# Attention layer on one core: the weighted sums of 8 heads in one run of the matrix engine instead of two runs of 4

## The chip, the core and the metric

One core of a Trainium2 chip runs the whole program. The time is the device time of one execution in microseconds (us). The engines are TensorE (PE), VectorE (DVE), ScalarE (ACT), GpSimd (POOL) and SyncE (SP, which only issues transfers).

## The reference

The input `x` is 8 sequences of 512 rows of 256. A first block (a small adapter with an expert matrix per sequence, a residual and a layer norm) is followed by a transformer layer with 16 heads of 16. Its attention adds a bias of 512 x 512 per head and masks columns:

```
x = _ln(src) * (1.0 + scale) + shift
scores = einsum('bhqd,bhkd->bhqk', q / sqrt(16), k) + attention_bias
scores = where(src_mask, -inf, scores)
ctx = einsum('bhqk,bhkd->bhqd', softmax(scores), v)
x = x + (ctx @ Wo + bo)
ff = _gelu2((_ln(x) * g2 + beta2) @ W1 + b1) @ W2 + b2
return x + ff
```

The weighted sums are the second `einsum`, `ctx`.

## The kernel before

**Tiling.** The 4096 rows are 16 chunks of 256 query rows (`NCH`, `CH`); a chunk is iteration `i`. A chunk has 16 heads x 2 halves of 128 queries = 32 score tiles of 128 x 512 (`TI`), one for each slot `t` of the iteration. Every engine has a program of its own, and all of them walk through the same slots.

**A score tile's way.** In slot `t` PE makes the scores (L823, bank `sc0` or `sc1`); DVE adds the masked bias and takes the maximum (L1371); ACT takes the exponential and its row sum (L996); three slots later (`LAG`), PE turns the tile in four transpositions (L830, bank `tp0` or `tp1`); ACT (L1002) or DVE (L1378, for the tiles in `DVE_MOVES`) copies it to `pT`. POOL has masked the bias earlier (L492). A score waits for the maximum of the tile two before it (L822), a turn for the exponential of its own tile and for the copy of the tile two before it (L827, L828). On ACT the copy of slot `t` (tile `t - 3`) stands ahead of the exponential of tile `t`; on DVE the maximum of tile `t` stands ahead of the copy.

**The weighted sums.** `pT` has two buffers of 4 heads (8 tiles, `TG`). `weigh(g)` (L777 to L791) takes one buffer: for 4 blocks of 128 keys and 4 heads it multiplies a 128 x 32 piece of `v_all` with a 128 x 256 piece of `pT`. The four heads stand in four column groups of the array (`tile_position`), so they run side by side. Even and odd groups of heads fill the two 16-row halves of each 32-row part of `pv[:, 0:256]`: the piece of `v_all` of an even group has its other 16 columns zero and the odd group adds. So two runs make one round `r` of 8 heads. In the profile a product of float32 shows as two records, so a run of 16 products has 32 records.

**Order around it.** Before, between and after the score and the turn of a slot (times `t.0`, `t.3`, `t.6`) each engine carries out other steps, whose slots are written in the tables `PE_AT`, `ACT_AT`, `DVE_AT`, `SP_AT`, `POOL_AT`, `MID` and `FFN` (L46 to L56). The runs of weighted sums stand on PE at 13.6, 21.6, 29.6 and, for the last group, 5.6 of the next iteration. Other steps on PE: `up` 0.3 (adapter), values 1.0 and 2.0, queries 8.6 and 10.0, transposition of the next rows `xm` 12.6, keys 15.6 and 16.3, `wo` 21.0 and 21.6, `ht` 28.6, and the feed-forward products in slots between. ACT: copy of the turned rows 14.0 (L859), queries 11.0 and 12.3, keys 17.0 and 18.0, a tanh at 5.0, 9.6, 14.3 and 19.0 (L957), `hT` 30.0. DVE: steps of two layer norms at 1.6 to 10.6 (ending in `xm`, L1110), gates of the feed-forward at 6.0, 10.3, 15.3, 19.6 (L1328), the output rows at 29.6 (L1335), the division of the weighted sums at 24.6 and 8.6 (L1349). POOL: inverse square roots at heads 6 and 8 of a chunk. SP loads the bias of head `n` after the turns of head `n - 8`. What an engine has in its list it does in that order; nothing overtakes.

**Waits of the weighted sums.** `weigh` waits for the copies of its 8 tiles, for `v_all`, and (first group of a round) for the division of the round before. It increments `pv_done`. The copies into a `pT` buffer wait until the run two groups back is done (L1001, L1377), the values' copy into `v_all` waits for the runs of the sequence two back (L1197), the division waits for the second run of its round (L1346). `spread_inverses` writes the other half of the bank of `pv` at 22.3 and 6.3 (4.0 in the last iteration).

Of the kernel before, what the change touches and what calls it, by code (L numbers as in the profile page):

```python
# [16 lines left out]
H, HD = 16, 16  # L17
# [3 lines left out]
CH = 256  # L21
NCH = B * S // CH
CT = D // P
FT = F // P
GH = 4
NG = H // GH
TI = 2 * H
TG = 2 * GH
KT = S // P
# [14 lines left out]


PE_AT = dict(up=0.3, v=(1.0, 2.0), q=(8.6, 10.0), xt1=12.6, k=(15.6, 16.3), down=(24.3, 25.3),  # L46
             pv=(13.6, 21.6, 29.6, 5.6), spread=(22.3, 6.3))
ACT_AT = dict(q=(11.0, 12.3), widen=(18.3, 2.3), spread=(23.6, 7.0), k=(17.0, 18.0), xT1=14.0, gelu=26.6)
DVE_AT = dict(x1=1.6, st0=2.3, mv0=2.6, v=3.0, n1=4.0, n2=6.3, st1=7.0, mv1=7.6, m1=8.3, m2=10.6, q=(11.6, 13.0),
              k=(17.6, 18.6), recip=(17.6, 1.6), ctx=(24.6, 8.6))  # L50
# [59 lines left out]
def wait(eng, sem, value):  # L110

    if value <= 0:
        return
    eng.wait_ge(sem, value)
# [7 lines left out]
def on_act(n):  # L122

    return n % TI not in (LAST_DVE_MOVES if n // TI == NCH - 1 else DVE_MOVES)


def moved(n, by_act):

    return sum(on_act(k) == by_act for k in range(n))


def head_of(hh):

    return 8 * (hh // 8) + 2 * (hh % GH) + hh // GH % 2
# [17 lines left out]
def build(nc, x, x_t, t_tok, e_tok, bias, mask, downT, upT, up_b, experts, gamma, beta,  # L152
# [16 lines left out]
    with ExitStack() as ctx:  # L169
        def sb(name, shape, dt=F32):  # L170
            return ctx.enter_context(nc.sbuf_tensor(name, shape, dt))

        def ps(name):
            return ctx.enter_context(nc.psum_tensor(name, [P, 512], F32))

        def sem(name):
            return ctx.enter_context(nc.semaphore(name))
# [26 lines left out]
        v_all = [sb(f"v_all{b}", [P, KT, HD + 2 * HD * H]) for b in range(2)]  # L204
        pT = [sb(f"pT{g}", [P, GH, KT, CH]) for g in range(2)]
# [58 lines left out]
        pv = ps("pv")  # L264
# [9 lines left out]
        def v_bank(c):  # L274
            return tp[1] if c == 0 else lb
# [34 lines left out]
        s = {n: sem(n) for n in names}  # L310
# [248 lines left out]
        def _(pe):  # L559
# [63 lines left out]
            def fold_expert(b, bank, j):  # L623
                return pe.matmul(bank[0:A + 1, j * D:(j + 1) * D], ew_t[:, b, :], up_w, start=True, stop=True)
# [23 lines left out]
            for b in range(6, 8):  # L648
                last = fold_expert(b, lc, b % 2)
# [24 lines left out]
            def body(i, attn, prev, nxt, pre, qv, down):  # L674
                a, c = i + 2, i + 1
                AT = PE_AT

                def norm_steps(t):
                    if pre and t == AT["up"]:
                        wait(pe, s["a_xt1"], a)  # L680
                        wait(pe, s["d_out"], i - 2)
                        adapter_up(a)
                    if qv and t in AT["q"]:
                        if t == AT["q"][0]:
                            pe.wait_ge(s["d_v"], c + 1)
                        queries(c, AT["q"].index(t))
                    if qv and t in AT["v"]:
                        if t == AT["v"][0]:
                            pe.wait_ge(s["a_xt1"], c + 1)
                            pe.wait_ge(s["d_k"], c + 1)  # L690
                            wait(pe, s["a_hT"], i - 1)
                        values(c, AT["v"].index(t))
                    if pre and t in AT["k"]:
                        if t == AT["k"][0]:
                            pe.wait_ge(s["a_xt1"], a + 1)
                            pe.wait_ge(s["d_q"], c + 1)
                        keys(a, AT["k"].index(t))
                    if pre and t == AT["xt1"]:
                        turn_rows(a)
                    if down and t in AT["down"]:  # L700
                        if t == AT["down"][0]:
                            wait(pe, s["d_act"], 4 * (i - 1))
                            pe.wait_ge(s["d_w1"], 1)
                        adapter_down((i + 3) // 2, AT["down"].index(t))
# [69 lines left out]
                        pe.wait_ge(s["d_hn"], m + 1)  # L774
                        transposes(lb, hn, "p_ht")

                def weigh(g):  # L777
                    gi = NG * i + g - (NG if g == NG - 1 else 0)
                    pe.wait_ge(s["copied_v"], moved(TG * (gi + 1), False))
                    pe.wait_ge(s["copied_a"], moved(TG * (gi + 1), True))  # L780
                    pe.wait_ge(s["d_v"], 2 * (gi // NG // 2) + 2)
                    if g % 2 == 0:
                        wait(pe, s["d_ctx"], gi // 2)
                    v = v_all[(gi // NG // 2) % 2]
                    for kt in range(KT):
                        for h in range(GH):
                            col = HD + 2 * HD * head_of(GH * g + h) - HD * (g % 2)
                            last = pe.matmul(pv[32 * h:32 * h + 32, 0:CH], v[:, kt, col:col + 2 * HD],  # L788
                                             pT[gi % 2][:, h, kt, :], start=(g % 2 == 0 and kt == 0),
                                             stop=(g % 2 == 1 and kt == KT - 1), tile_position=(0, 32 * h))  # L790
                    last.then_inc(s["pv_done"], 1)  # L791

                def spread_inverses(r):
                    ri = 2 * (i - r) + r
                    pe.wait_ge(s["a_wide"], ri + 1)
                    wait(pe, s["a_rin"], ri)
                    for j in range(2):
                        last = pe.transpose(inverse_bank(ri)[:, CH + j * P:CH + (j + 1) * P],
                                            rwide[:, j, :], ident[:, :])
                    last.then_inc(s["p_rin"], 1)  # L800

                def steps(t, at):
                    norm_steps(t)
                    if i == 1 and t in W1_AT["sums"]:
                        shift_sums(W1_AT["sums"].index(t))
                    for f in range(max(0, i - 2), min(i, NCH)):
                        ffn_steps(f, at)
                    if i > 0:
                        mid_steps(i - 1, at)
                    for g in range(NG):  # L810
                        if (prev if g == NG - 1 else attn) and t == AT["pv"][g]:
                            weigh(g)
                    for r in range(2):
                        if (prev if r else attn) and t == (4.0 if i == NCH else AT["spread"][r]):
                            spread_inverses(r)

                def score(t):
# [30 lines left out]
        def _(act):  # L848
# [83 lines left out]
            def body(i, attn, prev, nxt, pre, qv, down):  # L932
                a, c = i + 2, i + 1
                AT = ACT_AT
# [63 lines left out]

                def move(n):
                    act.wait_ge(s["pt_ready"], n + 1)  # L1000
                    wait(act, s["pv_done"], n // TG - 1)  # L1001
                    act.copy(pT[n // TG % 2][:, n // 2 % GH, :, (n % 2) * P:(n % 2 + 1) * P],  # L1002
                             tp[n % 2][:, :].rearrange("p (k q) -> p k q", k=KT)).then_inc(s["copied_a"], 1)

                for t in range(TI):
                    n = TI * i + t - LAG
# [7 lines left out]
        def _(dve):  # L1014
# [179 lines left out]
            def values(c):  # L1194
                b = c // 2
                dve.wait_ge(s["p_v"], c + 1)
                wait(dve, s["pv_done"], 2 * NG * (b - 1))  # L1197
                if c == 0:
                    dve.wait_ge(s["pool_chain"], 3)
                dst = v_all[b % 2][:, 2 * (c % 2):2 * (c % 2) + 2, HD:].rearrange("p j (h e) -> p j h e", e=2 * HD)  # L1200
                dve.tensor_tensor(dst[:, :, :, 0:HD],
                                  v_bank(c)[:, :].rearrange("p (j h d) -> p j h d", j=2, d=HD),
                                  bv_r[:, :].rearrange("p (h d) -> p h d", d=HD).unsqueeze(1).to_broadcast(
                                      [P, 2, H, HD]), ALU.add).then_inc(s["d_v"], 1)
# [43 lines left out]
            query_parts(0, 1)  # L1248
            dve.wait_ge(s["v_w_in"], 48)
            values(0)  # L1250
            shift_parts()
            for ft in range(FT):
# [4 lines left out]
            def body(i, attn, prev, nxt, pre, qv, down):  # L1257
                a, c = i + 2, i + 1
                AT = DVE_AT
# [83 lines left out]

                def divide(r):
                    ri = 2 * (i - r) + r
                    dve.wait_ge(s["pv_done"], 2 * ri + 2)  # L1346
                    dve.wait_ge(s["a_rin"], ri + 1)
                    wait(dve, s["p_wo"], i - r)
                    dve.tensor_tensor(ctxn[:, r, :], pv[:, 0:CH], rin[:, :], ALU.mult).then_inc(s["d_ctx"], 1)  # L1349
# [24 lines left out]

                def move(n):
                    dve.wait_ge(s["pt_ready"], n + 1)
                    wait(dve, s["pv_done"], n // TG - 1)  # L1377
                    dve.tensor_copy(pT[n // TG % 2][:, n // 2 % GH, :, (n % 2) * P:(n % 2 + 1) * P],  # L1378
                                    tp[n % 2][:, :].rearrange("p (k q) -> p k q", k=KT)).then_inc(s["copied_v"], 1)

                for t in range(TI):
                    n = TI * i + t - LAG
# [67 lines left out]
```

## Time and profile before

| | us |
|---|---|
| median of 3 runs | 959.73 (959.16 to 959.91) |
| profiled execution | 960.01 |
| its span, first to last instruction | 958.2 |
| PE busy | 890.0 (93%) |
| DVE busy | 703.1 (73%) |
| ACT busy | 703.9 (73%) |
| POOL busy | 702.8 (73%) |
| mean granted TensorE clock | 0.973 |

Busy time is the union of an engine's instructions; a matmul's end is modelled and overlaps the start of the next one, so what a product costs is best read from start to start. A step whose engine is idle much of the time costs nothing unless another engine waits for it. Idle time in brackets behind a row of the timeline names what the engine waited for. In a view by windows, the columns behind the window and its length are the busy times of PE, PEld (weight load), DVE, ACT and POOL (instructions in brackets), the granted TensorE clock, the share of the transfer engines and GB/s.

### The profile page before, as it was taken

How to read it: one execution, taken by the hardware profiler on the slowest of the kernel's cores; microseconds unless marked ns; L12 is line 12 of the kernel's file. 1: busy time of each engine (PE TensorE's matmuls, PEld its weight loads, DVE VectorE, ACT ScalarE, POOL GpSimd, SP SyncE). 2: the span in 40 equal slices, each digit the busy share in tenths (PEclk: the TensorE clock that was granted, in tenths of full speed). 3: DMA queues.
4: the chain of work that ended last, by engine and by line, in shares of the span. 5: the costliest groups of instructions: out<-in, count | busy, mean ns of one | idle time of the engine just before them, and what ended most of it. 6: DMA issues, size and time to landing. Idle time of an engine off the chain costs nothing. (4 is left out here: it accounts for less than half of the span.)

```text
span 958.2 us, 20699 instructions
## 1 busy us (share of the span) xinstructions
PE 890.0 (93%) x6472; PEld 659.6 (69%) x6472; DVE 703.1 (73%) x1901; ACT 703.9 (73%) x1667; POOL 702.8 (73%) x407
## 2 busy tenths in 40 slices
PE   3746889999999999999999999999999999999987
PEld 1425565777777776787777776787777777677765
DVE  4645787878778787878778787888778787675742
ACT  2435888978788787978788787978788787867641
POOL 1417997889788886978688886979788887885700
PEclk7877999999999999999999999999999999999998
DMA  5299969876897769776897769776897669765300
GB/s 158 79 263 335 293 221 256 241 237 200 254 290 206 230 210 255 238 238 198 249 291 209 231 208 270 228 238 200 245 267 214 220 195 274 238 192 166 100 12 11
DMA packets 147950, 207.41 MB, mean 216 GB/s; under 512 B 14385, under 2 KB 62322, under 8 KB 147842
## 3 DMA queue, kind: packets, MB, share of 16 engines
q1 hardware_dynamic: 145474, 204.12, 71.9%
q10 hardware_dynamic: 2368, 1.97, 0.8%
q8 instruction: 53, 0.87, 0.4%
q14 instruction: 55, 0.45, 0.2%
HBM read 185.05 MB, written 20.99 MB: 215 GB/s over the span
## 5 line engine op out<-in xcount | busy, mean ns | idle before, releaser
L492 POOL TENSOR_TENSOR bias_s<-mask_f,bias_s 128x1024 f32<-128x1024 f32 x256 | 601.2, 2372 | 132.5 <-DMA bias_s<-in_bias 132.2
L1371 DVE CUSTOM_DVE_ANT_0 bias_s<-sc,bias_s 128x512 f32<-128x512 f32 x512 | 347.6, 684 | 175.7 <-PE sc L823 165.3
L996 ACT ACTIVATE bias_s<-bias_s,mx 128x512 f32<-128x512 f32 x512 | 371.2, 725 | 91.4 <-DVE mx L1371 89.3
L830 PE MATMUL tp<-ident,bias_s 128*128 128x128 f32 x2048 | 311.5, 275 | 6.4 <-ACT pT L1002 3.4
L830 PEld LDWEIGHTS tp<-ident,bias_s 128*128 128x128 f32 x2048 | 252.1, 142 | 88.9 <-issue 15.0
L1002 ACT COPY pT<-tp 128x512 f32<-128x512 f32 x335 | 194.9, 582 | 100.6 <-PE tp L830 98.1
L823 PE MATMUL sc<-stk,stq 128*128 128x512 bf16 x512 | 196.4, 384 | 24.9 <-DVE mx L1371 14.2
L752 PE MATMUL la<-w_s,act_s 128*128 128x256 f32 x512 | 128.2, 380 | 0.2 <-DVE act_s L1328 0.2
L788 PE MATMUL pv<-pT,v_all 128*32 128x256 f32 x2048 | 124.3, 383 | 0.0
L1378 DVE COPY pT<-tp 128x512 f32<-128x512 f32 x177 | 121.1, 684 | 3.7 <-PE tp L830 3.6
L737 PE MATMUL lc<-hT,w_s 128*128 128x256 f32 x464 | 121.2, 385 | 2.5 <-ACT hT L951 1.9
L996 ACT ACTIVATION_READ_ACCUMULATOR bias_s<-bias_s,mx 128x1 f32 x512 | 98.4, 192 | 0.0
L823 PEld LDWEIGHTS sc<-stk,stq 128*128 128x128 bf16 x512 | 50.0, 98 | 66.5 <-issue 39.9
L752 PEld LDWEIGHTS la<-w_s,act_s 128*128 128x128 f32 x512 | 89.4, 190 | 8.4 <-DVE act_s L1328 0.4
L788 PEld LDWEIGHTS pv<-pT,v_all 128*32 128x32 f32 x2048 | 60.1, 110 | 49.0 <-issue 15.8
L737 PEld LDWEIGHTS lc<-hT,w_s 128*128 128x128 f32 x464 | 82.4, 193 | 12.9 <-ACT hT L951 2.5
L502 POOL TENSOR_SCALAR rs<-mv 128x2 f32<-128x2 f32 x48 | 9.3, 194 | 92.5 <-DVE mv L1105 90.1
L1328 DVE SCALAR_TENSOR_TENSOR act_s<-th,lc 128x512 f32<-128x512 f32 x57 | 39.0, 685 | 11.1 <-ACT th L957 10.8
L1371 DVE DVE_READ_ACCUMULATOR2_ANT mx<- 128x1 f32 x512 | 42.5, 83 | 0.0
L503 POOL TENSOR_TENSOR rs<-rs,powc 128x2 f32<-128x2 f32 x48 | 34.0, 708 | 4.0
L769 PE MATMUL lb<-wo_s,ctxn 128*128 128x256 f32 x128 | 33.0, 381 | 0.7 <-DVE ctxn L1349 0.7
L957 ACT ACTIVATE th<-lc 128x512 f32<-128x512 f32 x57 | 33.5, 587 | 0.0
(175 smaller groups left out, 797.1 us busy)
## 6 DMA issues: line engine op xcount, KB each, us to landing
bias_s<-in_bias SPq DMA_DIRECT2D x256, 512.0 KB, 4.6
stk<-k_parts SPq DMA_DIRECT2D x128, 96.0 KB, 3.9
stq<-q_parts SPq DMA_DIRECT2D x126, 96.0 KB, 4.1
k_parts<-kb SPq DMA_DIRECT2D x32, 192.0 KB, 2.3
q_parts<-qb SPq DMA_DIRECT2D x30, 192.0 KB, 2.4
xT<-in_x_t SPq DMA_DIRECT2D x8, 512.0 KB, 7.2
k_parts<-kb SPq DMA_DIRECT2D x32, 128.0 KB, 2.3
stk<-k_parts SPq DMA_DIRECT2D x64, 64.0 KB, 4.3
```

What stands on the lines that cost most here:

```text
L492: pool.tensor_tensor(tile, mask_f[:, :, :], tile, ALU.subtract).then_inc(s["masked"], 1)
L503: return pool.tensor_tensor(dst, dst, powc[:, :], ALU.pow)
L737: last = pe.matmul(h, w1_s[:, ct, ft * P:(ft + 1) * P], hT[:, ct, :], start=(ct == 0), stop=(ct == CT - 1))
L752: last = pe.matmul(rows, act_s[:, ft, j * P:(j + 1) * P], w2_s[:, ft, :], start=(ft == 0), stop=(ft == FT - 1))
L788: last = pe.matmul(pv[32 * h:32 * h + 32, 0:CH], v[:, kt, col:col + 2 * HD], pT[gi % 2][:, h, kt, :], start=(g % 2 == 0 and kt == 0), stop ...
L823: pe.matmul(sc[t % 2][:, :].rearrange("p (e k) -> p e k", e=2), stq[:, hh, j * P:(j + 1) * P], stk[:, :, hh, :], start=True, stop=True).th ...
L830: last = pe.transpose(tp[n % 2][:, kt * P:(kt + 1) * P], bias_s[:, n // 2 % NB, n % 2, kt * P:(kt + 1) * P], ident[:, :])
L996: act.activation(tile, tile, ACT.Exp, bias=mx[:, t:t + 1], scale=-1.0, accum_out=sums[:, j, head_of(hh):head_of(hh) + 1]).then_inc(s["prob ...
L1002: act.copy(pT[n // TG % 2][:, n // 2 % GH, :, (n % 2) * P:(n % 2 + 1) * P], tp[n % 2][:, :].rearrange("p (k q) -> p k q", k=KT)).then_inc( ...
L1328: dve.scalar_tensor_tensor(out=act_s[:, 2 * p:2 * p + 2, :].rearrange("p c n -> p (c n)"), in0=tanh_of(f, p), scalar=1.0, in1=w1_bank(f, p ...
L1371: dve.tensor_tensor_reduce(out=tile, in0=sc[t % 2][:, :], in1=tile, scale=1.0, scalar=BIG, op0=ALU.add, op1=ALU.min, accum_out=mx[:, t:t + ...
L1378: dve.tensor_copy(pT[n // TG % 2][:, n // 2 % GH, :, (n % 2) * P:(n % 2 + 1) * P], tp[n % 2][:, :].rearrange("p (k q) -> p k q", k=KT)).th ...
```

## The change

`weigh` takes a round of 8 heads: parts 0 and 1 (heads of `pT[0]`, then of `pT[1]`) one behind the other, 32 products in one run. It stands at 19.3 of its iteration and, for the second round, at 3.3 of the next. It waits for the copies of all 16 tiles. The very last round is split: its part 0 stands at 29.6 of the last chunk's iteration and its part 1 at 3.3 of the closing one. `pv_done` counts rounds instead of groups, and the waits on it are changed to match: a copy of tile `n` now waits for the round `n // 16` to be done. The inverses of the closing iteration stand on PE at 3.0 instead of 4.0.

```diff
 PE_AT = dict(up=0.3, v=(1.0, 2.0), q=(8.6, 10.0), xt1=12.6, k=(15.6, 16.3), down=(24.3, 25.3),
-             pv=(13.6, 21.6, 29.6, 5.6), spread=(22.3, 6.3))
+             pv=(19.3, 3.3), spread=(22.3, 6.3))
...
-                def weigh(g):
-                    gi = NG * i + g - (NG if g == NG - 1 else 0)
-                    pe.wait_ge(s["copied_v"], moved(TG * (gi + 1), False))
-                    pe.wait_ge(s["copied_a"], moved(TG * (gi + 1), True))
-                    pe.wait_ge(s["d_v"], 2 * (gi // NG // 2) + 2)
-                    if g % 2 == 0:
-                        wait(pe, s["d_ctx"], gi // 2)
-                    v = v_all[(gi // NG // 2) % 2]
-                    for kt in range(KT):
-                        for h in range(GH):
-                            col = HD + 2 * HD * head_of(GH * g + h) - HD * (g % 2)
-                            last = pe.matmul(pv[32 * h:32 * h + 32, 0:CH], v[:, kt, col:col + 2 * HD],
-                                             pT[gi % 2][:, h, kt, :], start=(g % 2 == 0 and kt == 0),
-                                             stop=(g % 2 == 1 and kt == KT - 1), tile_position=(0, 32 * h))
-                    last.then_inc(s["pv_done"], 1)
+                def weigh(ri, parts=range(2)):
+                    r, turned = ri % 2, TG * (2 * ri + parts[-1] + 1)
+                    pe.wait_ge(s["copied_v"], moved(turned, False))
+                    pe.wait_ge(s["copied_a"], moved(turned, True))
+                    pe.wait_ge(s["d_v"], 2 * (ri // 4) + 2)
+                    wait(pe, s["d_ctx"], ri)
+                    v = v_all[(ri // 4) % 2]
+                    for e in parts:
+                        for kt in range(KT):
+                            for h in range(GH):
+                                col = HD + 2 * HD * head_of(GH * (2 * r + e) + h) - HD * e
+                                last = pe.matmul(pv[32 * h:32 * h + 32, 0:CH], v[:, kt, col:col + 2 * HD],
+                                                 pT[e][:, h, kt, :], start=(e == 0 and kt == 0),
+                                                 stop=(e == 1 and kt == KT - 1), tile_position=(0, 32 * h))
+                    if parts[-1] == 1:
+                        last.then_inc(s["pv_done"], 1)
...
-                    for g in range(NG):
-                        if (prev if g == NG - 1 else attn) and t == AT["pv"][g]:
-                            weigh(g)
                     for r in range(2):
-                        if (prev if r else attn) and t == (4.0 if i == NCH else AT["spread"][r]):
+                        if (prev if r else attn) and t == AT["pv"][r]:
+                            weigh(2 * (i - r) + r, range(1, 2) if r and i == NCH else range(2))
+                    if i == NCH - 1 and t == 29.6:
+                        weigh(2 * i + 1, range(1))
+                    for r in range(2):
+                        if (prev if r else attn) and t == (3.0 if i == NCH else AT["spread"][r]):
                             spread_inverses(r)
...
                 def move(n):
                     act.wait_ge(s["pt_ready"], n + 1)
-                    wait(act, s["pv_done"], n // TG - 1)
+                    wait(act, s["pv_done"], n // (2 * TG))
...
-                wait(dve, s["pv_done"], 2 * NG * (b - 1))
+                wait(dve, s["pv_done"], NG * (b - 1))
...
-                    dve.wait_ge(s["pv_done"], 2 * ri + 2)
+                    dve.wait_ge(s["pv_done"], ri + 1)
...
                 def move(n):
                     dve.wait_ge(s["pt_ready"], n + 1)
-                    wait(dve, s["pv_done"], n // TG - 1)
+                    wait(dve, s["pv_done"], n // (2 * TG))
```

## Rows read from the trace of the kernel before

**Rows 1.** The page, part 1: busy us, share of the span, instructions.

```profile
PE 890.0 (93%) x6472; PEld 659.6 (69%) x6472; DVE 703.1 (73%) x1901; ACT 703.9 (73%) x1667; POOL 702.8 (73%) x407
```

**Rows 2.** Windows, one per chunk (0, 1, 8, 14, 15): length, then busy times, clock.

```profile
58.60:115.20 56.60, 42.87 (x278) 28.75 (x279) 35.88 (x99) 34.92 (x88) 40.49 (x22) 0.82 1.01 308
115.20:167.80 52.60, 48.14 (x354) 31.10 (x354) 42.09 (x115) 43.99 (x102) 46.16 (x27) 1.00 0.84 243
...
490.75:543.35 52.60, 52.23 (x402) 40.22 (x401) 42.64 (x116) 42.42 (x105) 44.80 (x26) 1.00 0.76 233
810.90:862.00 51.10, 49.73 (x386) 37.44 (x385) 36.11 (x96) 40.10 (x100) 41.61 (x21) 1.00 0.72 222
862.00:926.90 64.90, 61.93 (x444) 47.73 (x443) 39.04 (x100) 43.42 (x105) 31.47 (x16) 1.00 0.33 100
```

**Rows 3.** Waits of PE from 170 to 811 us: in total, times, longest.

```profile
PE la L563 <- DVE xm L1110: 3.9, 12, 0.3
```

**Rows 4.** Timeline of PE around a run (chunk 8): start, us, engine, line, operation.

```profile
511.96 1.03 PE L737 MATMUL lc<-hT,w_s 128*128 128x256 f32 x4
512.92 1.93 PE L788 MATMUL pv<-pT,v_all 128*32 128x256 f32 x32
514.79 0.39 PE L823 MATMUL sc<-stk,stq 128*128 128x512 bf16 x1
```

**Rows 5.** Timeline of three engines, slots 3 to 12.6 of chunk 8.

```profile
496.38 0.60 PE L830 MATMUL tp<-ident,bias_s 128*128 128x128 f32 x4
...
498.15 0.73 ACT L996 ACTIVATE bias_s<-bias_s,mx 128x512 f32<-128x512 f32 x1 [0.54 <-DVE mx L1371]
...
500.26 0.57 ACT L957 ACTIVATE th<-lc 128x512 f32<-128x512 f32 x1
...
506.29 0.69 DVE L1371 CUSTOM_DVE_ANT_0 bias_s<-sc,bias_s 128x512 f32<-128x512 f32 x1
...
509.02 0.87 DVE L1110 SCALAR_TENSOR_TENSOR xm<-la,rs,mod 128x256 f32<-128x256 f32 x2
...
509.95 0.66 PE L563 MATMUL la<-ident,xm 128*128 128x128 f32 x4 [0.33 <-DVE xm L1110]
```

**Rows 6.** Timeline of three engines, slots 13 to 19 of chunk 8.

```profile
513.01 0.68 DVE L1371 CUSTOM_DVE_ANT_0 bias_s<-sc,bias_s 128x512 f32<-128x512 f32 x1
...
514.46 0.56 ACT L859 COPY xT<-la 128x512 f32<-128x512 f32 x1
...
516.10 1.03 PE L589 MATMUL lb<-xT,wk_s 128*128 128x256 f32 x4
...
521.08 0.60 PE L830 MATMUL tp<-ident,bias_s 128*128 128x128 f32 x4
...
521.52 1.03 PE L752 MATMUL la<-w_s,act_s 128*128 128x256 f32 x4
...
522.14 0.59 ACT L1002 COPY pT<-tp 128x512 f32<-128x512 f32 x1
...
522.38 0.38 PE L823 MATMUL sc<-stk,stq 128*128 128x512 bf16 x1
```

**Rows 7.** Timeline of DVE and ACT behind the run at 21.6 of chunk 8.

```profile
529.47 0.69 DVE L1371 CUSTOM_DVE_ANT_0 bias_s<-sc,bias_s 128x512 f32<-128x512 f32 x1 [2.19 <-PE sc L823]
...
529.98 0.59 ACT L1002 COPY pT<-tp 128x512 f32<-128x512 f32 x1 [2.46 <-PE tp L830]
```

**Rows 8.** Timeline of DVE and PE from slot 29.6 of chunk 8 to slot 0.

```profile
541.22 0.68 DVE L1335 SCALAR_TENSOR_TENSOR outb<-la,x2s 128x512 f32<-128x512 f32 x1
...
542.50 0.69 DVE L1371 CUSTOM_DVE_ANT_0 bias_s<-sc,bias_s 128x512 f32<-128x512 f32 x1 [0.60 <-PE sc L823]
...
543.35 0.38 PE L823 MATMUL sc<-stk,stq 128*128 128x512 bf16 x1
```

## The prediction

> **What bounds the kernel now.** I read the page's busy times first: PE 93% of the span, VectorE (DVE) and ScalarE (ACT) 73% each [rows 1]. Then the windows by chunk [rows 2]: in a steady chunk (52.6 us here, 54.9 with an adapter product) PE is busy 52.2 us, ACT 42.4, DVE 42.6; chunk 0, chunk 1 and chunk 14 leave PE idle 13.7, 4.5 and 1.4 us. Then PE's waits over twelve steady chunks [rows 3]: 3.9 us in 641 us, all one wait of 0.3 us a chunk for `xm`. So PE sets the pace, and the others keep up. What matters is how narrowly: a score is allowed two slots ahead of its maximum, a transposed tile two ahead of its copy, so ACT and DVE can lag PE by about two slots and no more.
>
> **What the change removes.** Each run of weighted sums has an entry and an exit. In [rows 4] the product before the run starts at 511.96; four records of that size take 0.86 to 0.87 us start to start (521.52 to 522.38 in [rows 6]), 0.216 each, so the run could start at 512.825 and starts at 512.92: 0.095 us. From there, eight rounds of four heads at 0.216 us are 1.73 us, so the next score could start at 514.65 and starts at 514.79: 0.14 us. A run costs 1.97 us, of which 0.235 us is its two edges. Before there are 64 runs, after 33 (31 whole ones and the last one in two halves): 31 x 0.235 = 7.3 us less work for PE. The Trainium skill, "TensorEngine Tiling (Array Packing)", Key Properties, says that a change of tiling mode drains the engine; the trace agrees (the edges above). By that rule alone the change gains those 7.3 us; that is the first rival.
>
> **What it adds.** No arithmetic, no transfer, no instruction but fewer waits. It puts 16 rounds in one place: 16 x 0.216 + 0.235 = 3.69 us. The transposition of the next tile (16 or 0) is queued behind the run on PE, the next score behind that; at slot 3 ACT has the copy of tile 0 ahead of its next exponential, so ACT soon stands idle, and DVE gets no new score. The two tile buffers no longer alternate, but the copies don't wait for `pv_done`: PE turns tile 16 only after the run is over. The cost is elsewhere: the four old runs (slots 5.6, 13.6, 21.6, 29.6) were pauses in which ACT and DVE caught up. Where they had no slack, a pause taken away gives PE nothing. I follow chunk 8 through its four stretches [rows 5 to 8].
>
> Slots 3 to 12.6 (run at 5.6 gone) [rows 5]. The turn of tile 0 starts at 496.38; PE gets to the transposition of `xm` at 509.95. The chain to `xm`: tanh at 500.26 on ACT, the gate on DVE, then DVE without a pause (nine groups of instructions, none with idle time ahead) up to the maximum at 506.29, the exponential after it and the second tanh on ACT, its gate, `xm` at 509.02, PE at 509.95. From the first tanh that is 9.69 us, nearly all work. The first tanh is 3.88 us behind the turn of tile 0. In the new order the maximum of tile 3 is done during the run, so the 0.54 us that ACT waited at 498.15 falls away and tanh comes at 3.34 us. PE then waits until 3.34 + 9.69 - 0.06 = 12.97 us, against 13.57 before. Gain 0.60 of 1.97 us. (An earlier wait, of tile 4's turn for the copy of tile 2, lies within this one: PE would be there at 3.7 us, the copy, behind that tanh, ends at 4.4.)
>
> Slots 12.6 to 19.3 (run at 13.6 gone) [rows 6]. DVE is packed until the maximum at 513.01; its exponential follows, then the copy of the turned rows, from 514.46 to 515.02, and the key product at 516.10 needs it. Without the run PE would be there at 514.13, now at 515.06: gain 1.04. Then the run itself waits for the copy of tile 15: turn at 521.08, copy at 522.14 because a key conversion is ahead of it on ACT, its end at 522.73, while PE is done with the score at 522.60 and could enter at 522.69. The run enters near 522.81: 0.12 lost. Gain 0.92.
>
> Slots 19.3 to 29.6 (run at 21.6 gone) [rows 7]. DVE had 2.19 us and ACT 2.46 us idle around that run, and are rested by the run before. Tile 16's copy and the gate behind it on DVE cost 1.2 us, before the next score is in. Gain the full 1.97. Bounds: 0.9, if that start is worse than I read it, and 1.97.
>
> Slots 29.6 to 3.3 (run at 29.6 gone) [rows 8]. DVE is packed (maximum, copy, maximum, copy, output row at 541.22). The maximum that follows sat 0.60 us idle until 542.50 for a score; now it starts at 541.83, ends 0.70 later, and the first score of the next chunk, which needs it, starts at 542.55 in place of 543.35. Gain 0.80.
>
> Sum of a steady chunk: the removed pauses give back 0.60 + 0.92 + 1.97 + 0.80 = 4.29 us; the two runs at 3.3 and 19.3 cost 2 x 3.69 = 7.38. The chunk gets **3.09 us longer**, though PE has 0.47 us less to do.
>
> The ends, bounded from rows 2 and the same reasoning. Chunk 0 has no run at slot 3, PE idles 13.7 us anyway, and three runs (5.9 us) turn into one: +1.5, between 0 and 4. Chunk 1 has PE idle already, so its pauses give back less: +4, between 3 and 5.5. Chunk 14 prepares no chunk, its DVE is less loaded (36.1 of 51.1 us [rows 2]): +1.6, between 0.5 and 3. Chunk 15 prepares nothing at all, PE is busy 61.9 of 64.9 us and ACT 43.4 [rows 2], and its last run stays split: -0.5. The tail waits for the same last copy, then one half run as before: 0. Sum: 1.5 + 4 + 12 x 3.09 + 1.6 - 0.5 = 43.7 us on the profiled execution's 960.0 (span 958.2), so 1003.7; the median of the runs is 0.3 lower: **1003.4 us**.
>
> Covered at nothing: POOL's masks (44.8 of 52.6 us busy, with a longer chunk to do them in), the SP queue's loads (a tile is loaded long before its score), the inverses and divisions, whose runs end earlier than before (19.3 for 21.6, 3.3 for 5.6) with their own slots unchanged. If POOL's cover went, its price would be at most its idle time, 7.8 us a chunk, spread over waits that DVE hardly has today. The granted clock is 1.00 in all steady chunks and 0.82 in chunk 0 [rows 2], where PE idles most; a shift there may cost or give 2 us, which is in the range.
>
> **The rivals.**
>
> *The slack is enough, only the edges count.* For it: DVE and ACT are idle a fifth of every chunk, and PE shows no wait for them [rows 1 to 3]. Then it ends at 960.0 - 7.3 - 0.3, about 952.4 us. It decides if the new waits stay under 0.47 us a chunk. Against it: the chain of rows 5 has hardly any idle time in it for 9.7 us, and PE already waits at its end. Chance 0.07; 0.01 that gain and waits cancel within 0.2%. The skill's "Perfetto Trace Analysis" tells to take the engine with the most occupied time as the bottleneck; that points to this rival, and the rows of rows 5 are why I don't follow it.
>
> *One stretch binds, the others don't.* If ACT and DVE use the long run better than I read (less queued behind tile 16's and tile 0's copies), only slots 3 to 12.6 cost: +1.37 - 0.47 = 0.9 us a chunk, about 14 us in all: 974 us. Chance 0.14.
>
> *The gap after a long run spreads.* If ACT and DVE start each stretch too far behind, the one I count as a full gain gives back nothing either: 7.38 - 2.32 = 5.06 us a chunk, 12 x 5.06 + 7 = 68: 1028 us. Chance 0.10.
>
> *Nothing changes.* The code does what it says: one `start` and one `stop` per region of `pv`, the waits consistent. The order on PE is fixed by hand, so the runs can't stay apart. Chance under 0.01, within the 0.01 above.
>
> **How the numbers follow.** Forecast 0.68, with 985 to 1018 for itself (0.8 us a chunk either way and the ends' bounds). The range takes in most of the second rival's upper half: 978 to 1019. About 0.2% (1.9 us) is what a measurement of this kernel can tell from no change: faster 0.07, same 0.01, slower 0.92.
>
> **What would show it.** In the profile after: 33 runs, whole ones of 3.69 us start to start, PE busy some 7 us less in sum and idle some 50 us more; a steady chunk of about 55.7 us (58 with the adapter product). Waits of PE that are new: the turn of tile 4 on the copy of tile 2 (0.6 to 0.8 us), the rows of `xm` (about 1.3 in sum with it), the key product on ACT's copy of the turned rows (0.7), score 0 on DVE's maximum (0.8), the run at 19.3 on the copy of tile 15 (0.1). ACT and DVE idle about 3 us in each long run. Wrong would be: chunks under 54 us (the slack is there), or PE waiting in slots 20 to 29 as well (the gap spreads).

## The result and the profile after

| | before | after |
|---|---|---|
| median of the runs | 959.82 us (4 runs) | 1014.74 us (4 runs, 1011.95 to 1018.15) |
| ratio, 95% interval | | 1.0563, 1.0536 to 1.0591 |
| profiled execution, span | 960.01, 958.2 us | 1018.15, 1016.4 us |

The change makes the kernel 54.9 us slower; forecast was 43.6 us (1003.4, range 978 to 1019). The profiled execution is the slowest of its four, so its sums come to 58.2 us.

The page of the kernel after, parts 1 and 5 (busy us, share, count; in part 5 the idle time of PE before a group and what ended it):

```profile
PE 905.1 (89%) x6472; PEld 668.8 (66%) x6472; DVE 703.3 (69%) x1901; ACT 698.1 (69%) x1667; POOL 703.0 (69%) x407
...
L834 PE MATMUL tp<-ident,bias_s 128*128 128x128 f32 x2048 | 313.4, 276 | 33.0 <-ACT pT L1006 17.8
L827 PE MATMUL sc<-stk,stq 128*128 128x512 bf16 x512 | 196.2, 384 | 30.8 <-DVE mx L1375 18.5
L789 PE MATMUL pv<-pT,v_all 128*32 128x256 f32 x2048 | 119.0, 384 | 4.0 <-issue 3.1
L589 PE MATMUL lb<-xT,wk_s 128*128 128x256 f32 x120 | 32.2, 392 | 8.5 <-ACT xT L863 8.5
```

No engine has more to do: the counts are those of [rows 1], DVE is as busy as before and ACT 5.8 us less. PE waits now: before turns 33.0 us (before the change 6.4), before scores 30.8 (24.9), before keys 8.5 (0.5). The run itself is cheaper: its group is busy 119.0 us, where it was 124.3. That PE shows 905 us busy in place of 890 is no added work either; the last section comes back to it.

Windows by chunk of the kernel after (0, 1, 8, 14, 15), to be held against [rows 2]:

```profile
63.10:120.90 57.80, 41.64 (x247) 28.41 (x247) 35.71 (x99) 34.84 (x88) 42.71 (x23) 0.85 0.94 290
120.90:178.40 57.50, 48.45 (x353) 31.37 (x354) 42.00 (x115) 43.42 (x101) 44.16 (x26) 1.00 0.83 243
...
521.90:578.00 56.10, 53.15 (x402) 40.67 (x401) 42.75 (x116) 42.63 (x107) 43.17 (x26) 1.00 0.70 210
862.70:916.30 53.60, 50.17 (x385) 37.52 (x385) 35.91 (x96) 39.68 (x99) 40.86 (x21) 1.00 0.69 203
916.30:984.50 68.20, 64.00 (x476) 48.79 (x476) 39.21 (x100) 43.36 (x104) 32.17 (x16) 1.00 0.32 97
```

Every steady chunk is longer by the same amount: 56.1 us for 52.6 (even), 58.3 for 54.9 (odd). The granted clock is 1.00 in all of them, as before; it plays no part.

**The stretches.** I cut a chunk at four points on PE: the start of tile 0's turn, of the transposition of `xm`, of tile 16's turn, and of the score of tile 29. The same cut is made in every trace below. (From the rounded times of [rows 5] the first stretch before comes to 13.57 us.)

| stretch (chunk 8; odd chunk 9 in brackets) | before | after | difference | forecast |
|---|---|---|---|---|
| turn 0 to rows | 13.56 (13.56) | 12.88 (12.88) | -0.68 | -0.60 |
| rows to turn 16, with the run at 19.3 | 12.65 (12.65) | 15.55 (15.55) | +2.90 | -0.92 + 3.69 = +2.77 |
| turn 16 to score 29 | 16.73 (19.03) | 14.81 (17.11) | -1.92 | -1.97 |
| score 29 to turn 0, with the run at 3.3 | 9.66 (9.66) | 12.72 (12.93) | +3.06 (+3.27) | -0.80 + 3.69 = +2.89 |
| chunk | 52.60 (54.90) | 55.95 (58.47) | +3.35 (+3.57) | +3.09 |

Now the rows behind it. Timeline of three engines, kernel after, from the run at 3.3 to the rows of chunk 8; it answers to [rows 5]:

```profile
527.85 3.66 PE L789 MATMUL pv<-pT,v_all 128*32 128x256 f32 x64
...
531.44 0.66 PE L834 MATMUL tp<-ident,bias_s 128*128 128x128 f32 x4
...
532.13 0.59 ACT L1006 COPY pT<-tp 128x512 f32<-128x512 f32 x1 [3.66 <-PE tp L834]
...
533.35 0.69 DVE L1375 CUSTOM_DVE_ANT_0 bias_s<-sc,bias_s 128x512 f32<-128x512 f32 x1 [3.07 <-PE sc L827]
...
534.85 0.59 ACT L961 ACTIVATE th<-lc 128x512 f32<-128x512 f32 x1
...
536.06 0.63 PE L834 MATMUL tp<-ident,bias_s 128*128 128x128 f32 x4 [0.69 <-ACT pT L1006]
...
540.74 0.68 DVE L1375 CUSTOM_DVE_ANT_0 bias_s<-sc,bias_s 128x512 f32<-128x512 f32 x1
...
543.38 0.63 PE L834 MATMUL tp<-ident,bias_s 128*128 128x128 f32 x4 [0.39 <-ACT pT L1006]
543.39 0.87 DVE L1114 SCALAR_TENSOR_TENSOR xm<-la,rs,mod 128x256 f32<-128x256 f32 x2
...
544.32 0.66 PE L563 MATMUL la<-ident,xm 128*128 128x128 f32 x4 [0.31 <-DVE xm L1114]
```

ACT and DVE stand idle 3.66 and 3.07 us in the run. The first tanh comes 3.41 us behind the turn of tile 0 (3.88 before; forecast 3.34), and from it to the rows it takes 9.47 us (9.69 before). PE meets that chain three times: tile 4's turn waits 0.69 us, tile 9's 0.39 (a wait that was not forecast), the rows 0.31.

Timeline of three engines, kernel after, slots 13 to 19 of the same chunk, to be held against [rows 6]:

```profile
548.82 0.56 ACT L863 COPY xT<-la 128x512 f32<-128x512 f32 x1
...
549.44 1.13 PE L589 MATMUL lb<-xT,wk_s 128*128 128x256 f32 x4 [0.49 <-ACT xT L863]
...
554.52 0.60 PE L834 MATMUL tp<-ident,bias_s 128*128 128x128 f32 x4
...
555.58 0.59 ACT L1006 COPY pT<-tp 128x512 f32<-128x512 f32 x1
...
555.82 0.38 PE L827 MATMUL sc<-stk,stq 128*128 128x512 bf16 x1
...
556.27 3.66 PE L789 MATMUL pv<-pT,v_all 128*32 128x256 f32 x64
...
559.86 0.66 PE L834 MATMUL tp<-ident,bias_s 128*128 128x128 f32 x4
```

The keys wait for the copy of the rows, and the run starts 0.45 us behind the score, where a run that waits for nothing starts 0.31 behind one (0.216 and the edge of 0.095): 0.14 for the copy of tile 15, forecast 0.12. From its start to the next turn the run takes 3.59 us; with its entry edge 3.69, as forecast.

Slots 29 to 0 of the same chunk, to be held against [rows 8], and, in the first three rows, the odd chunk before it (ACT and PE, slots 26.6 to 30):

```profile
516.56 1.28 ACT L856 ACT_TABLE_LOAD   x1
...
518.56 1.28 ACT L1000 ACT_TABLE_LOAD   x1
...
520.72 0.66 PE L834 MATMUL tp<-ident,bias_s 128*128 128x128 f32 x4 [1.17 <-ACT bias_s L1000]
...
576.57 0.68 DVE L1339 SCALAR_TENSOR_TENSOR outb<-la,x2s 128x512 f32<-128x512 f32 x1
...
577.16 0.68 DVE L1375 CUSTOM_DVE_ANT_0 bias_s<-sc,bias_s 128x512 f32<-128x512 f32 x1
...
578.00 0.38 PE L827 MATMUL sc<-stk,stq 128*128 128x512 bf16 x1 [0.58 <-DVE mx L1375]
```

In the even chunk score 0 waits for the maximum behind the output rows, as forecast. In the odd chunk it is another resource that holds PE: the adapter's gelu makes ACT load two function tables of 1.28 us, the exponential of tile 27 is late, and its turn waits 1.17 us. Before, with the run at 29.6, the loads cost nothing: the stretch is 9.66 us in even and odd chunks.

### The profile page after: what moved, and what is told of

Read it like the earlier page. It is cut to its first block and busy times, and to the rows that moved or that the text cites. A ratio compares the mean times of both kernels' runs of the same rounds, so it can differ in the third digit from the quotient of the medians.

```text
span 1016.4 us, 20669 instructions
## 1 busy us (share of the span) xinstructions
PE 905.1 (89%) x6472; PEld 668.8 (66%) x6472; DVE 703.3 (69%) x1901; ACT 698.1 (69%) x1667; POOL 703.0 (69%) x407
## 3 DMA queue, kind: packets, MB, share of 16 engines
q10 hardware_dynamic: 2368, 1.97, 0.7%
## 5 line engine op out<-in xcount | busy, mean ns | idle before, releaser
L834 PEld LDWEIGHTS tp<-ident,bias_s 128*128 128x128 f32 x2048 | 244.8, 141 | 135.4 <-issue 56.9
L827 PE MATMUL sc<-stk,stq 128*128 128x512 bf16 x512 | 196.2, 384 | 30.8 <-DVE mx L1375 18.5
L789 PE MATMUL pv<-pT,v_all 128*32 128x256 f32 x2048 | 119.0, 384 | 4.0 <-issue 3.1
L789 PEld LDWEIGHTS pv<-pT,v_all 128*32 128x32 f32 x2048 | 69.7, 111 | 52.0 <-issue 19.1
L589 PE MATMUL lb<-xT,wk_s 128*128 128x256 f32 x120 | 32.2, 392 | 8.5 <-ACT xT L863 8.5
```

The lines of the kernel that those rows point to most:

```text
L827: pe.matmul(sc[t % 2][:, :].rearrange("p (e k) -> p e k", e=2), stq[:, hh, j * P:(j + 1) * P], stk[:, :, hh, :], start=True, stop=True).th ...
L834: last = pe.transpose(tp[n % 2][:, kt * P:(kt + 1) * P], bias_s[:, n // 2 % NB, n % 2, kt * P:(kt + 1) * P], ident[:, :])
```

## Experiments

All times are medians; ratios are to the kernel before, measured on the same chip. "Stretches" are the four lengths of the table, chunk 8.

**1 and 2: one round merged at a time.**

```diff
-             pv=(13.6, 21.6, 29.6, 5.6), spread=(22.3, 6.3))
+             pv=(19.3, 19.3, 29.6, 5.6), spread=(22.3, 6.3))
```

> The kernel before with only the first round of a chunk merged: both of its runs stand back to back at 19.3, the runs at 29.6 and 5.6 stay. Theory (what is lost is the pauses in stretches where ACT and DVE have no slack, and each stretch has its own price): the two stretches that this round touches cost 15.55 - 12.65 = +2.90 us and 14.81 - 16.73 = -1.92 us in the traces of before and after, so +0.98 us a chunk, about +15 us: 975 us (970 to 980). Rival (a long run of PE starves ACT and DVE by itself, wherever it stands): half of the whole loss of 55 us, 987 us. Rival (only the edges of runs count, the loss is elsewhere): 16 edges fewer, 956 us.

```diff
...
-                    for g in range(NG):
-                        if (prev if g == NG - 1 else attn) and t == AT["pv"][g]:
-                            weigh(g)
+                    for g in range(2):
+                        if attn and t == AT["pv"][g]:
+                            weigh(g, False)
+                    if prev and i < NCH and t == 3.3:
+                        weigh(2, True)
+                        weigh(3, True)
...
```

> The kernel before with only the second round of a chunk merged: both of its runs stand back to back at 3.3 of the next chunk, the runs at 13.6 and 21.6 stay; the last round stays as it was. Theory (each stretch has its own price): 12.88 - 13.56 = -0.68 us in slots 3 to 12.6 and about 12.79 - 9.66 = +3.13 us from slot 29 to the next turn of tile 0, so +2.45 us a chunk, 15 rounds, about +37 us: 997 us (990 to 1002). Rival (a long run starves ACT and DVE by itself): 987 us. Rival (only edges count): 956 us.

Measured: first round merged 977.21 us, 1.0171 (1.0137 to 1.0206); second round merged 993.87 us, 1.0337 (1.0305 to 1.0370). Stretches 13.56, 15.41, 14.81, 9.72 and 12.88, 12.65, 16.73, 12.65. The two losses (17 and 34 us) are not alike, and together make 51 of the 55 us. Each touches only its own two stretches, and these have the lengths of the kernel after to within 0.14 us (15.41 for 15.55 the widest). So the loss goes by the place, not by the number of long runs.

**3: `xm` ahead of the gate.**

```diff
-DVE_AT = dict(x1=1.6, st0=2.3, mv0=2.6, v=3.0, n1=4.0, n2=6.3, st1=7.0, mv1=7.6, m1=8.3, m2=10.6, q=(11.6, 13.0),
+DVE_AT = dict(x1=1.6, st0=2.3, mv0=2.6, v=3.0, n1=4.0, n2=6.3, st1=7.0, mv1=7.6, m1=8.3, m2=10.3, q=(11.6, 13.0),
...
-FFN = dict(hT=30.0, w1=(3.0, 4.0, 8.0, 9.0, 13.0, 13.6, 17.6, 18.3), tanh=(5.0, 9.6, 14.3, 19.0),
+FFN = dict(hT=30.0, w1=(3.0, 4.0, 8.0, 9.0, 13.0, 13.6, 17.6, 18.3), tanh=(5.0, 10.3, 14.3, 19.0),
```

> The changed kernel with two steps moved in slots 9.6 to 10.6: DVE makes xm (10.3) ahead of the second gate (10.3, behind it) instead of after it, and ACT's second tanh goes from 9.6 to 10.3, behind the copy of tile 7. Theory: the rows' transposition waits for xm in that order only because the gate waits for the tanh; it comes up to 0.97 us earlier, but the next stretch is bound by DVE's maxima and ACT's copy of the turned rows, which come only 0.33 us earlier, so most of it is given back: -0.33 to -0.5 us a chunk, about 1009 us (1005 to 1013). Rival (the long run itself is the loss): no change, 1014 to 1015. Rival (PE paced by this wait alone): -0.97 us a chunk, 1001.

Measured 1015.36 us, 1.0574 (1.0525 to 1.0623), against 1.0563 for the changed kernel: nothing gained. Stretches 11.94, 16.42, 14.81, 12.65: the rows come 0.94 us earlier, and the next stretch is 0.87 us longer. PE's timeline in that kernel, slot 15 of chunk 8:

```profile
546.90 0.39 PE L827 MATMUL sc<-stk,stq 128*128 128x512 bf16 x1 [0.49 <-DVE mx L1375]
547.13 0.60 PE L834 MATMUL tp<-ident,bias_s 128*128 128x128 f32 x4
548.22 1.13 PE L589 MATMUL lb<-xT,wk_s 128*128 128x256 f32 x4 [0.49 <-ACT xT L863]
```

PE came earlier and waited more: now also for DVE's maximum of tile 13, and then for ACT's copy as before. My expectation of 1009 us (1005 to 1013) missed: I counted 0.33 us for DVE's packed list being started earlier and got 0.07. A wait on the bound engine is not a price; what it shields has to be free too.

**4: the copy of the turned rows ahead of an exponential.**

```diff
-ACT_AT = dict(q=(11.0, 12.3), widen=(18.3, 2.3), spread=(23.6, 7.0), k=(17.0, 18.0), xT1=14.0, gelu=26.6)
+ACT_AT = dict(q=(11.0, 12.3), widen=(18.3, 2.3), spread=(23.6, 7.0), k=(17.0, 18.0), xT1=13.3, gelu=26.6)
```

> The changed kernel with ACT's copy of the turned rows moved from 14.0 to 13.3, ahead of the exponential of tile 13 that waits for its maximum. Theory: the key product waits 0.49 us for this copy (its start 0.65 us later than PE could); with the copy done, that wait is gone and no other stands in its place at once: -0.5 to -0.65 us a chunk, about 1006 us (1003 to 1010). Rival (the long run itself, or the entry wait at 19.3 behind the key conversions takes it over): no change, 1013 to 1015.

Measured 1006.87 us, 1.0473 (1.0436 to 1.0510), 8 us under the changed kernel. The second stretch is 14.79 for 15.55 us, the others are unchanged, and the keys' wait is gone. So this wait was a price by itself, as forecast; per chunk it was 0.76 us where I had 0.5 to 0.65.

**5: the output rows later.**

```diff
-PE_AT = dict(up=0.3, v=(1.0, 2.0), q=(8.6, 10.0), xt1=12.6, k=(15.6, 16.3), down=(24.3, 25.3),
+PE_AT = dict(up=0.6, v=(1.0, 2.0), q=(8.6, 10.0), xt1=12.6, k=(15.6, 16.3), down=(24.3, 25.3),
...
-           gate=(6.0, 10.3, 15.3, 19.6), w2=(19.0, 20.0, 23.6, 24.6, 25.6, 26.0, 27.0, 28.0), out=29.6, store=31.0)
+           gate=(6.0, 10.3, 15.3, 19.6), w2=(19.0, 20.0, 23.6, 24.6, 25.6, 26.0, 27.0, 28.0), out=30.6, store=31.3)
```

> The changed kernel with DVE's output rows moved from 29.6 to 30.6, behind the maximum of tile 30 (and the adapter product on PE, which waits for them, from 0.3 to 0.6). Theory: score 0 waits 0.58 us for that maximum, because the output rows stand ahead of it; DVE's next pause is what the removed run at 29.6 used to give. -0.6 to -0.65 us a chunk, 13 to 14 chunks, about 1006 us (1003 to 1010). Rival (the wait moves on to the adapter product or to the next maximum, since DVE's work in these slots is the same): -0.2 us a chunk or less, 1012 to 1015.

Measured 1016.37 us, 1.0563 (1.0519 to 1.0608): no gain, where 1006 was expected. The last stretch is 12.46 us in even chunks (0.26 less in chunk 8) and 13.79 in odd ones (0.87 more). In even chunks score 0 waits no longer, but the turn behind it waits 0.22 us for ACT's copy. PE and ACT of that kernel, end of odd chunk 7 (the trace's next rows after ACT's two table loads):

```profile
521.54 0.66 PE L834 MATMUL tp<-ident,bias_s 128*128 128x128 f32 x4 [1.17 <-ACT bias_s L1000]
...
523.28 0.56 ACT L1006 COPY pT<-tp 128x512 f32<-128x512 f32 x1
...
523.99 0.30 PE L834 MATMUL tp<-ident,bias_s 128*128 128x128 f32 x1 [0.88 <-ACT pT L1006]
```

The wait of 1.17 us for the exponential is that of the changed kernel; a second one of 0.88 follows, for a copy, since ACT has not caught up and the adapter product (0.86 us of PE's own work) no longer stands ahead of the turn. The rival was right that the wait moves on; in odd chunks the reason seems to be ACT's table loads. Run 11 tests that reason.

**6: the three together.** The edits of 3, 4 and 5 on the changed kernel.

> The changed kernel with all three: xm ahead of the gate and the tanh later, ACT's copy of the turned rows at 13.3, the output rows at 30.6. Theory: xm first gave nothing alone because score 15 then waits for DVE's maximum and the keys for the copy; the copy's part is worth 0.76 us a chunk, the output rows' 0.6, xm first still nearly nothing: -1.4 us a chunk, about 996 us (991 to 1001). Rival (the parts add fully, 0.9 + 0.76 + 0.6): 985. Still slower than before in both cases: outside of its two long runs PE has about 45 us of work a steady chunk, and DVE and ACT have over 39 us to do beside it.

Measured 1007.75 us, 1.0497 (1.0460 to 1.0534). Stretches 11.95, 15.65, 14.81, 12.45, and 13.79 for the last one in odd chunks: -1.10 us in even chunks, +0.03 in odd ones. `xm` first again gives 0.93 and costs the next stretch nearly that. The miss against 996 us is mostly that of experiment 5, whose gain I had counted in.

**7: the same three moves on the kernel before.**

> The kernel before (four runs) with the same three moves. Theory: here the only wait of PE in a steady chunk is for xm (its start about 0.5 us late, shown as 0.3 us idle), and the run at 13.6 gives the next stretch its slack, so the gain of xm first isn't given back: -0.4 to -0.5 us a chunk, 13 chunks, about 954 us (952 to 957). The other two moves do nothing here. Rival (the chain of DVE and ACT is as tight here and gives it back, as in the changed kernel): 960.

Measured 961.02 us, 1.0002 (0.9988 to 1.0017). Stretches 12.96, 12.99, 16.73, 9.66 (10.10 in odd chunks): `xm` first gives 0.60 and 0.34 comes back; odd chunks lose 0.44 in the last stretch. The expectation of 954 us missed: it had the moves of 4 and 5 at nothing. Experiment 10 has neither, and its odd chunks lose nothing, so the 0.44 comes from these moves. PE's waits of 0.3 us for ACT's copy, from 220 to 860 us, are five here and two before, which points to the turn that the adapter product at 0.6 no longer covers, as in experiment 5; no run separates it.

**8: one merged round with the two moves that could help it.** Experiment 1 with the edits of 3 and 4.

> The kernel with only the first round merged (977 us), with xm first and ACT's copy of the turned rows at 13.3. Theory: the copy is worth 0.76 us a chunk as in the changed kernel, and xm first is given back to DVE's maximum of tile 13: 13 x 0.76 = 10 us, 967 us (963 to 971). Rival (with the pause at 5.6 still there xm first counts as well): another 0.4 us a chunk, 961 us, level with before.

Measured 967.65 us, 1.0081 (1.0049 to 1.0113). Stretches 12.97, 15.49, 14.81, 9.66. The number is as forecast, in part by luck: against experiment 1 a chunk gains 0.60 in the first stretch and loses 0.08 in the second, 0.52 us in all, where the theory had 0.76.

**9: PE's own work where the pause was.** On the kernel of experiment 8:

```diff
-           gate=(6.0, 10.3, 15.3, 19.6), w2=(19.0, 20.0, 23.6, 24.6, 25.6, 26.0, 27.0, 28.0), out=29.6, store=31.0)
+           gate=(6.0, 10.3, 15.3, 19.6), w2=(15.0, 19.0, 23.6, 24.6, 25.6, 26.0, 27.0, 28.0), out=29.6, store=31.0)
```

> As the kernel with the first round merged and the two moves in slots 9.6 to 13.3 (968 us), and in addition the feed-forward's second product starts one step earlier: its first piece at 15.0 instead of 19.0, its second at 19.0 instead of 20.0. So PE has 0.86 us of its own work where it waited for DVE and ACT since the run at 13.6 is gone, and 0.86 us less right behind the long run, where the other engines are rested. Theory (what is lost is what PE waits in that stretch, not the run's length): 0.6 to 0.9 us a chunk less, 13 chunks, 957 to 960 us, level with before or just under it. Rival (the long run starves ACT and DVE, wherever PE's other work stands): 966 to 969.

Measured 970.99 us, 1.0108 (1.0086 to 1.0130): no gain; it is even above the rival's 966 to 969, and far from the 957 to 960 of the theory. Stretches 12.96, 16.46, 13.95, 9.73: the third is 0.86 shorter, the second 0.97 longer. PE's waits from 230 to 860 us, of this kernel and then of experiment 8 (in total, times, longest):

```profile
PE la L752 <- ACT xT L859: 5.5, 11, 0.5
```

```profile
PE sc L823 <- DVE mx L1371: 5.8, 12, 0.5
```

The product that I moved needs the bank that ACT's copy of the turned rows frees, so it waits for ACT as long (0.5 us) as the score behind it waited for DVE. It stands behind the wait, not in it: it fills nothing. What could fill it would have to need neither engine; I found no such step and left it there.

**10: `xm` first alone, on the kernel before.** The edit of 3 on the kernel before.

> The kernel before with xm made ahead of the second gate and the second tanh at 10.3, nothing else. In the trace of before with all three moves the stretch to the rows is 0.60 us shorter and the next 0.34 us longer in even and odd chunks alike, while the adapter product at 0.6 costs odd chunks another 0.44. Without that: -0.26 us a chunk, 957 us (956 to 959). Rival (it is all given back as in the changed kernel): 960.

Measured 957.68 us over 12 runs, 0.9974 (0.9956 to 0.9992). Stretches 12.97, 12.99, 16.72, 9.66 (52.35 us for 52.60). This is the fastest kernel of the study, by 0.26%, about what can be told from nothing.

**11: experiment 5 without the function tables.**

```diff
-                act.activation(h2[0:A, :], lc[0:A, :], ACT.Gelu, bias=vec[0:A, VEC["down_b"]:VEC["down_b"] + 1]
+                act.activation(h2[0:A, :], lc[0:A, :], ACT.Gelu if b < 2 else ACT.Tanh, bias=vec[0:A, VEC["down_b"]:VEC["down_b"] + 1]
```

> The changed kernel with the output rows at 30.6 and the adapter product at 0.6 (1016 us), and with the adapter's gelu of sequences 2 to 7 replaced by tanh, so that ACT loads no other table at slot 26.6 of odd chunks (two loads of 1.28 us); the computation differs in that function. Theory (that move failed because in odd chunks ACT's table loads, not DVE, bind slots 29 to 3): odd chunks lose their 13.79 - 12.46 = 1.33 us, 6 chunks, -8 us: 1008 us (1005 to 1011). Rival (the tables are covered): 1016.

Measured 1008.98 us, 1.0505 (1.0470 to 1.0540). This kernel computes another function for sequences 2 to 7. The last stretch is 12.46 us in even and in odd chunks, all 12 table loads inside the chunks are gone, and the activation itself takes as long as before (0.67 us for 0.69). So the 1.33 us of an odd chunk in experiment 5 are ACT's table loads.

**12: a short run, elsewhere.**

```diff
-             pv=(13.6, 21.6, 29.6, 5.6), spread=(22.3, 6.3))
+             pv=(18.3, 21.6, 29.6, 5.6), spread=(22.3, 6.3))
```

> The kernel before, four short runs, with only the first of them moved from 13.6 to 18.3. No run is longer than before, no edge is saved, and PE's work between the same two points is the same. Theory (what is lost is the pause in slots 13 to 15): the keys again wait for the copy behind DVE's packed maxima, the stretch from the rows to tile 16 is 12.65 + 0.93 = 13.6 us, and the others unchanged: +0.9 us a chunk, 13 to 14 chunks, 972 us (969 to 975). Rival (the length of a run is what starves ACT and DVE): 960 us, no change.

Measured 978.65 us, 1.0178 (1.0151 to 1.0204). Stretches 13.56, 13.74, 16.73, 9.66. Nothing is merged here, no run is longer, and the loss is that of experiment 1 (16.8 us for 17.4). PE's timeline in slots 14 and 15 of this kernel, chunk 8:

```profile
522.94 0.39 PE L823 MATMUL sc<-stk,stq 128*128 128x512 bf16 x1
523.17 0.60 PE L830 MATMUL tp<-ident,bias_s 128*128 128x128 f32 x4
524.26 1.13 PE L589 MATMUL lb<-xT,wk_s 128*128 128x256 f32 x4 [0.49 <-ACT xT L859]
```

And the waits of PE from 230 to 860 us, the same three lines in this kernel and, digit for digit, in that of experiment 1:

```profile
PE lb L589 <- ACT xT L859: 5.4, 11, 0.5
PE la L563 <- DVE xm L1110: 3.6, 11, 0.3
PE tp L830 <- DVE pT L1378: 1.1, 2, 0.9
```

This settles the question between the two theories: the loss in this stretch is the missing pause at 13.6, not the length of the run. Merging even helps a little: the stretches of experiment 1 sum to +0.84 us a chunk over before and those of this one to +1.09, and the 0.25 between them is about the two edges (0.235) that the merge saves. It also shows that the forecast of 972 us was too low; the stretch costs 1.09 us where I had 0.93, and chunk 15 loses 1.8 us too (66.81 for 64.99 us from its first score to the last turn).

## Why the prediction was right, and where it was off

**The mechanism.** Right. A run of PE is also a pause for the engines that feed it, and where they have no slack, taking the pause away gives PE nothing. It is shown by 1 and 2 (the loss belongs to places), by 12 (the place without the length gives the same waits), and by 4 and 11 (taking one named cause away gives about its forecast share). For the second round, which makes two thirds of the loss, no run moves short runs without merging them; there the part of the pauses is argued from the waits and from experiment 2.

**The edges.** Right: 0.235 us each; a run of 8 heads takes 3.69 us from the score before it to the turn after it, less that score's own 0.216. "PE busy some 7 us less in sum" was wrong: the run's group is 5.3 us less busy, PE as a whole 15 us more; its idle time grew by 43 us, not 50.

**A steady chunk.** The whole came to +54.9 us for +43.6, and the steady chunks have the largest share of that miss, 4.1 us in twelve. Forecast +3.09, measured +3.35 in even and +3.57 in odd chunks. Term by term: slots 3 to 12.6, -0.60 against -0.68; slots 12.6 to 19.3, +2.77 against +2.90; slots 19.3 to 29.6, -1.97 against -1.92; slots 29.6 to 3.3, +2.89 against +3.06 and +3.27. Only the last has a cause that I had missed: I followed chunk 8 and took it for all, and an odd chunk has the table loads. Its share is small, 0.2 us in six chunks, since the wait for DVE hides most of them; it became 1.3 us as soon as experiment 5 took the cover away. The remaining 0.1 to 0.2 us a stretch I take for the start-up of products behind a wait (last section), which my sums left out; no run separates it. A small thing that I read past: in [rows 3]'s view PE has one more wait, 0.3 us once, of a turn for ACT's copy.

**The ends.** From the starts of the chunks' first scores in the two traces:

| | forecast | measured |
|---|---|---|
| up to chunk 0's first score | 0 | +4.5 |
| chunk 0 | +1.5 | +1.1 |
| chunk 1 | +4 | +4.9 |
| chunks 2 to 13 | +37.1 | +41.2 |
| chunk 14 | +1.6 | +2.5 |
| chunk 15 | -0.5 | +3.2 |
| tail | 0 | +0.7 |

I don't count the first row as the change's: the set-up code is the same in all kernels, and in the traces of this study chunk 0 starts anywhere between 58.6 and 63.2 us. The profiled execution was 3.4 us over its median; whether that excess lies in this row is not shown, since a kernel has one trace. The one step that failed is **chunk 15**, "-0.5". I had it save two edges. But it gives up three pauses (3 x 1.97 us), since its last round stays split, and takes in two long runs (7.38): +1.5 us on paper. And I let PE's 61.9 of 64.9 us stand for a chunk in which nothing else binds. From score to score, slots 14, 15 and 23 are 1.2, 0.6 and 0.55 us longer in the trace after and slot 4 is 0.7 shorter, which with the 1.5 makes the 3.2. PE's waits there are for DVE: turns for its copies 1.4 us (0.4 before), a score for its maximum 0.6 (none before).

**The rivals.** "The slack is enough" rested on occupied time: DVE and ACT idle a fifth of every chunk. They did, and the kernel lost 5.6%. The Trainium skill, "Perfetto Trace Analysis", Identifying the Most-Contended Engine, takes the engine with the highest occupancy as the bottleneck. By plain busy time that is PE here, before and after (93 and 89%), and the rule says nothing on what a pause of PE is worth. The same section wants TensorE's headroom judged by other shares, among them that of the weight loads; that is 69% before and 66% after, under the 73 and 69% of ACT and DVE. "One stretch binds" was wrong, three do; "the gap spreads" was wrong, the stretch behind slot 19.3 gave back 1.92 of 1.97 us. Of the waits forecast by name all five are there: tile 4's turn (0.69), the rows (0.31), the keys (0.49 for 0.7), score 0 (0.58 for 0.8), the run at 19.3 (0.14). Not forecast were tile 9's turn (0.39), tile 28's (0.30, for DVE's copy) and, in odd chunks, tile 27's (1.17).

## What to carry to other kernels

In a kernel that the busiest engine paces by hand-written order, a block of its work is also a rest for the others. Before moving or merging such a block, look at the rows of the other engines over the stretch that loses it: in this kernel the three stretches whose rows had little idle time ahead of them gave back 0.6 to 0.8 of the 1.97 us of a pause, and the one with 2.19 and 2.46 us of it gave back 1.92. Then check every kind of iteration, since a rarely used step (here a table load) can sit in the same slack.

## What the runs showed that I had not expected

**Busy time that is no work.** PE did the same products with fewer edges between them (7.3 us less) and shows 905 us busy for 890. A product is shown at its whole length, and the next one usually starts before that is over: the records of a transposition start every 0.11 us and show 0.27. Where a wait follows, nothing covers the last 0.16 us. So the keys start 0.65 us later than PE could have been there: 0.49 is shown as idle, and 0.16 as the record ahead of the wait. The trace after has 162 idle gaps of PE, of any length, and that of before 77; 85 x 0.16 us is an estimate of 14 us. The rest I have not separated; some of it is that a group behind a wait can take longer to get going (the keys' reads 1.13 us for 1.03). Where PE waits often, its idle time in the profile is too small and its busy time too large; start to start is the measure.

**A wait can move without changing.** In experiments 3 and 9 one wait went away and another of the same length took its place within two slots (0.94 us given, 0.87 taken; 0.86 and 0.97). In the kernel before, with its pause, the same move kept 0.26 of 0.60 us.

**Spread.** The changed kernel's four runs lie 6.2 us apart (1011.95 to 1018.15), those of before in the same comparison 1.4 us. Why is open. Between kernels, the traces start chunk 0 up to 4.6 us apart with the same set-up code; whether one kernel's runs differ there is not shown.
